# Smoothing factors earlier in SyncE's queue, and five pieces of the last stages moved

## The chip, the cores and the metric

The kernel runs on one core of one Trainium2 chip. The metric is the device time of one execution in microseconds (us). Engines are named as in the profile: PE is the matrix engine (PEld its weight loads), DVE the vector engine, ACT the scalar engine, POOL the GpSimd engine, SP the engine that only issues transfers here (SPq its queue).

## The reference, cut to what matters

Input x is [4, 256, 256] (batch, sequence, feature), and so is the context. Four residual blocks follow one another:

```
x = x + wkv(layernorm(x), context)                 # a scan over the sequence
x = x + quantised_linear(layernorm(x))             # 256 x 256, 8 bit
x = x + L1_xattn(layernorm(x), context)            # below: most of the work
x = x + L1_ffn(layernorm(x))                       # the last layer
```

```
ln_out = ln(h); xq = fp8(clip(ln_out / in_scale))  # one xq for each of q, qx, k, v
q, qx  = ln(xq @ wq), ln(xq @ wqx)                 # 16 heads of 128, 8 groups of 2
k, v   = ln(xq @ wk), xq @ wv                      # 8 groups
kx, vx = ln(context @ w_kv_x[k]), context @ w_kv_x[v]
core   = softmax(q k^T / sqrt(128)) v              # and the same with qx, kx, vx
cat    = fp8(clip(concat(core, xout) / proj_smooth))
x      = x + (cat @ wproj) * scale                 # 4096 features back to 256
```

`L1_ffn` runs along the batch axis of 4: layer norm, a convolution of two steps, SiLU, projections to q, k, v, g, a routed linear attention, a norm by head, a gate, and a projection back.

## The kernel before, in words

**Units.** The attention block is cut into 32 units: unit `u` is batch `u // 8` and group `u % 8` (`b, g = divmod(u, G)`). In each unit two heads of self attention (x = 0) and two of cross attention (x = 1) are computed for two halves (t = 0, 1) of the sequence. Each engine has its own program, a loop over units, and semaphores tie them together. The order of instructions is written by hand.

**PE in iteration u.** `scores(u, 0, 0)` (L625, L626), the second half of the projections of unit u + 1 (`project(u + 1, 1)`, L521 and L529), the other scores, and four times `weigh` (L638: probabilities times values). Between them stand the transposes of unit u + 1 (`turn`, L594), the rough scores from which its row maxima come (`guard`, L611), and the first half of the projections of unit u + 2 (`project(u + 2, 0)`). `turn_outputs(u - 1)` (L652) turns the outputs of the unit before. Once in eight units `project_out` (L662) multiplies the collected outputs with the weights; its second half and the turning of outputs share one PSUM bank, XB, and `residual` on DVE (L1586) reads that bank and frees it.

**DVE in iteration u.** `quantise(u - 1)` (L1577 to L1581), a piece of preparation for the next batch (`early`), `outputs(u, 0, 0)` (L1563 and L1565: divide by the row sum and by the smoothing factors), `normalise(u + 1, 1)` (L1531, L1533), `outputs(u, 0, 1)`, where g is 1 the `residual` of the batch before, another piece of preparation (`middle`), the bf16 copies `halves(u + 1)` (L1542, L1544), `outputs(u, 1, 0)`, the row maxima (`maxima`, L1551), `outputs(u, 1, 1)`, a last piece (`end`), and two more maxima. `weigh` writes all four results of a unit to one bank, OB, so each `weigh` waits until `outputs` has read the one before it (`o_evac`).

**Preparation.** The first two blocks of the next batch run in slices beside the units of the batch before: `ahead(u)` gives batch and step. Step 4 (units 3, 11, 19) adds the first block to x, takes the statistics in `early` and applies them in `middle` (`ln_apply`, L1291). Step 6 (units 5, 13, 21) adds the second block and takes the statistics in `early` (L1349, L1281 to L1286), POOL raises the variance to the power -1/2 (L1121), and `middle` applies it.

**Transfers.** SP issues nearly all of them, in the order of its program, and stands at each wait until it is met. In iteration u it waits for the outputs of unit u - 2, loads the smoothing factors of unit u (`ism`, L366, two buffers), then waits for the projections of unit u and loads the projection weights of unit u + 2 (`WQ`, L341, 1.5 MB, two buffers). The weights come from a DRAM copy, `wq_split`: in the first eight units they are prepared on the side (`weights`, `low_weights`, L492 to L500, L891, L1512) and stored there (L329), and the loads of raw weights (L306, L321) stand in the same queue.

**POOL in iteration u.** `diagonals(u, 0)` (L1175), which `scores(u, 0, 0)` waits for, the powers for the head norms of unit u + 1 (L1161), `diagonals(u, 1)`, the norms of the preparation, and `half(u + 1)` (L1168), which `guard(u + 1, 1)` waits for.

**The end.** The last layer's statistics of three of the four batches (`stats3`, L1635 to L1640, on DVE) stand in iteration 30 behind `outputs(30, 1, 1)`, ahead of the last maxima of unit 31. POOL's `power3` (L1196) stands ahead of `half(31)` in the same iteration. DVE then applies them (`normalise3`, L1646), and PE turns the three results (`turn_inputs3`, L707) between the scores of unit 31, all in bank QB[1], each waiting for ACT's copy (`turned3`, L985) of the one before. `project3` (L724) begins the last layer's projections behind the last `weigh` of unit 31.

Of the kernel before, what the change touches and what calls it, by code (L numbers as in the profile page):

```python
# [7 lines left out]
ALU = mybir.AluOpType  # L8
# [34 lines left out]
def build_program(nc, a, out):  # L43
# [28 lines left out]
    with main:  # L72
# [20 lines left out]
        mhalf = sb("mhalf", [P, 16])  # L93

# [71 lines left out]
        st3 = lb("st3", [P, T8, 6])  # L166
        mv3 = lb("mv3", [P, T8, 2])
        ve3 = lb("ve3", [P, T8])
        pw3 = lb("pw3", [P, T8])
# [74 lines left out]
        T3B, P3A, P3B, OT3B, OUT3B = QB[1], (QB[0], QB[2]), QB[3], (QB[1], SB[1]), (OB, XB)  # L244
# [46 lines left out]
        def _(sp):  # L291
# [39 lines left out]

            def load_weights(u):

                g = u % G
                sp.wait_ge(s["qkv_done"], 4 * (u - 1))
                if u < G:
                    sp.wait_ge(s["wq01_stored"], 32)
                    sp.wait_ge(s["wq_stored"], 16 * (g - 1))
                else:
                    sp.wait_ge(s["wq_stored"], 16 * (G - 2))  # L340
                sp.dma_start(WQ[u % 2][:].bitcast(F32).rearrange("p a k c -> p (a k c)"), wq_dram[g]).then_inc(s[f"wq{u % 2}_loaded"], 16)  # L341
# [13 lines left out]
            sp.wait_ge(s["smooth_stored"], 16)  # L355
            sp.wait_ge(s["xq4_ready"], 4)
# [5 lines left out]
            for u in range(UNITS):  # L362
                g = u % G
                if u >= 2:
                    sp.wait_ge(s["o_evac"], 4 * (u - 1))
                sp.dma_start(ism[:, u % 2], smooth_dram.rearrange("(x f) -> x f", x=2)[:, g * HPG * P:(g + 1) * HPG * P]  # L366
                             .partition_broadcast(P)).then_inc(s[f"ism{u % 2}_loaded"], 16)
                if u + 2 < UNITS:
                    load_weights(u + 2)
                if u == 0:  # L370
                    store_weights(4)
                if u == 1:
                    weights(6)
                if u == 2:
                    store_weights(5)
                    weights(7)
                if u == 3:
                    store_weights(6)
                    load_out_weights(0)
                if u == 4:  # L380
                    store_weights(7)
                if u == 5:
                    load_out_weights(2)
                    load_out_weights(4)
                if u == 6:
                    load_out_weights(6)
                if u and ahead(u) and ahead(u)[1] == 0:
                    b = ahead(u)[0]
                    sp.wait_ge(s["xq4_ready"], 4 * b)
                    sp.dma_start(craw, cv_[b]).then_inc(s["ctx_loaded"], 16)  # L390
# [16 lines left out]
        def _(pe):  # L407
# [293 lines left out]
            def turn_inputs3(l):  # L701

                pe.wait_ge(s["h3_ready"], l + 1)
                pe.wait_ge(*(s["h3T_evac"], l) if l else (s["max_ready"], 4 * UNITS))
                for c in range(KT):
                    for t in range(NT):
                        last = nc.tensor.transpose(T3B[:, (c * NT + t) * P:(c * NT + t + 1) * P],  # L707
                                                   h3[:, l * NT + t, c * P:(c + 1) * P], ident[:])
                last.then_inc(s["h3T_done"], 1)

            def project3(l):

                if l == 0:
                    pe.wait_ge(s["w3_loaded"], 80)
                pe.wait_ge(s["silu_ready"], l + 1)
# [32 lines left out]
            for u in range(UNITS - 1):  # L748
# [39 lines left out]
                for r in round_of(u, 2):  # L788
                    weights(*r)
                guard(u + 1, 1)  # L790
# [5 lines left out]
            turn_inputs3(0)  # L796
            scores(u, 0, 0)
            turn_inputs3(1)
            scores(u, 0, 1)
            turn_inputs3(2)  # L800
# [22 lines left out]
        def _(act):  # L823
# [159 lines left out]
            def turned3(l):  # L983
                act.wait_ge(s["h3T_done"], l + 1)
                A(hT[:, :, l, :], T3B[:].rearrange("p (k t) -> p k t", k=KT), ACT.Copy).then_inc(s["h3T_evac"], 1)  # L985
# [69 lines left out]
            turned3(0)  # L1055
            exps(u, 0, 0)
            turned3(1)
            exps(u, 0, 1)
            turned3(2)
# [36 lines left out]
        def _(pool):  # L1096
# [102 lines left out]
            for u in range(UNITS):  # L1199
# [21 lines left out]
                if u == UNITS - 2:  # L1221
                    power3(0, B - 1, 1)
                if u + 1 < UNITS:
                    half(u + 1)

# [44 lines left out]
        def _(dve):  # L1270
# [32 lines left out]
            def early(b, step):  # L1303
# [43 lines left out]
                if step == 6:  # L1347
                    for t in range(NT):
                        ch.add(v.scalar_tensor_tensor(out=xs[:, b, t, :], in0=hb[:, t, :], scalar=fq[:, 4, t:t + 1],  # L1349
                                                      in1=xs[:, b, t, :], op0=ALU.mult, op1=ALU.add))  # L1350
                    ch.wait()

                    ln_stats(b, 2, 1.0 + EPS, EPS * EPS)
                if step == 7:
                    fp8(b, (0, 1))

# [249 lines left out]
            early(0, 6)  # L1606
# [124 lines left out]
            for u in range(UNITS - 1):  # L1731
# [12 lines left out]
                outputs(u, 0, 1)  # L1744
                if g == 1 and b:
                    residual(b - 1)
                if nb:
                    middle(nb, step)
                for r in round_of(u, 0):
                    low_weights(*r)  # L1750
                halves(u + 1)
                outputs(u, 1, 0)
                maxima(u + 1, 0, 0)
                maxima(u + 1, 0, 1)
                outputs(u, 1, 1)
                for r in round_of(u, 1):
# [3 lines left out]
                if u == UNITS - 2:  # L1760
# [5 lines left out]
                if u == UNITS - 2:  # L1766
                    normalise3(0, B - 1, 1)

# [73 lines left out]
```

## Time and profile before

| | us |
|---|---|
| median of 3 runs | 782.08 |
| lowest and highest | 781.76, 784.39 |
| the profiled execution | 781.98 |
| its span | 780.3 |
| PE busy | 649.8 (83%) |
| DVE busy | 567.3 (73%) |
| ACT busy | 421.1 (54%) |
| POOL busy | 264.5 (34%) |

Span is the time from the first to the last instruction of the core; 1.7 us of the profiled execution lie outside it. Busy shares are means over the whole span. Matmul ends are modelled. A unit takes 16.7 us where no preparation runs beside it, and 17 to 26 us elsewhere.

### The profile page before, as it was taken

Reading aid. Unit: us, or ns where it says so; the run is one execution under the profiler, and the core shown is the slowest. Engines: PE = TensorE matmul, PEld = TensorE weight load, DVE = VectorE, ACT = ScalarE, POOL = GpSimd, SP = SyncE. Lnnn points to the kernel's source line nnn. Section 1 sums busy time; section 2 is a strip of 40 time slices with the busy share of each in tenths; the row PEclk is TensorE's granted clock in tenths of the full one; section 3 lists DMA queues with packets and bytes.
Section 4 is the critical chain, followed back from the end, with each engine's and each line's share of the span. In section 5 each row is a group of like instructions: output and inputs, shape, how many; then the busy total and the mean of one; then the engine's idle time right before and its main releaser. Section 6 shows DMA issues by size and latency. Waiting matters only on the chain.

```text
span 780.3 us, 12837 instructions
## 1 busy us (share of the span) xinstructions
PE 649.8 (83%) x4241; PEld 513.0 (66%) x4279; DVE 567.3 (73%) x1361; ACT 421.1 (54%) x1362; POOL 264.5 (34%) x346
## 2 busy tenths in 40 slices
PE   4258769977889999999899899998998999869444
PEld 2247657755767777877687778776786787646233
DVE  7985558957567757877978588778645666667995
ACT  4156647745657736566665456676645666542221
POOL 3014343323213443434235434343322333224260
PEclk9567999989989999999999999999999999979668
DMA  8157274463456222233232233333421430200001
GB/s 250 54 217 228 96 233 174 179 199 116 164 150 214 96 86 95 98 101 101 100 104 95 83 105 98 95 123 90 152 85 38 148 112 15 81 0 2 0 1 54
DMA packets 33212, 86.47 MB, mean 111 GB/s; under 512 B 2911, under 2 KB 28155, under 8 KB 28283
## 3 DMA queue, kind: packets, MB, share of 16 engines
q1 hardware_dynamic: 32960, 85.63, 33.4%
q8 instruction: 35, 0.57, 0.3%
q14 instruction: 31, 0.25, 0.1%
q10 hardware_dynamic: 186, 0.02, 0.0%
HBM read 71.99 MB, written 13.65 MB: 110 GB/s over the span
## 4 chain that ended last, share of the span: by engine, by line
PE 57%; DVE 24%; DMA 7%; issue 5%; ACT 4%; SPq 1%; POOL 1%; DVEq 0%; POOLq 0%; ACTq 0%
PE bank L638 14%; PE bank L521 12%; PE bank L625 9%; PE bank L529 6%; DMA ism<-smooth_inverse 6%; DVE Cb L1565 4%; PE bank L594 3%; PE bank L662 3%; PE bank L724 2%; PE bank L626 2%; PE bank L611 1%; PE bank L652 1%; DVE ro L1563 1%; DVE stage L1512 1%; DMA wq_split<-stage 1%
## 5 line engine op out<-in xcount | busy, mean ns | idle before, releaser
L638 PEld LDWEIGHTS bank<-V,Pt 128*128 128x128 f32 x1024 | 130.5, 196 | 71.9 <-DVE Cb L1565 60.1
L638 PE MATMUL bank<-V,Pt 128*128 128x129 f32 x1024 | 145.0, 286 | 36.3 <-DVE Cb L1565 34.4
L925 ACT ACTIVATE square<-bank 128x128 bf16<-128x128 f32 x384 | 101.5, 277 | 92.5 <-PE bank L521 54.0
L521 PE MATMUL bank<-WQ,xq 128*128 128x256 f32 (+1 forms) x1024 | 136.7, 286 | 3.9 <-DVE xq L1453 2.7
L521 PEld LDWEIGHTS bank<-WQ,xq 128*128 128x128 f32 x1024 | 127.3, 193 | 17.0 <-DVE nm L1551 9.8
L625 PE MATMUL bank<-QT,KTt 128*128 128x512 f32 x256 | 133.5, 603 | 1.6 <-POOL diag L1175 1.6
L908 ACT ACTIVATE Pt<-bank 128x512 f32<-128x512 f32 x128 | 76.8, 600 | 73.5 <-remote 46.7
L1551 DVE TENSOR_REDUCE nm<-bank 128x2 f32<-128x512 f32 x128 | 82.1, 683 | 45.4 <-PE bank L611 45.3
L1161 POOL TENSOR_TENSOR rs<-ve,mhalf 128x6 f32<-128x6 f32 x64 | 95.0, 1485 | 5.3
L1175 POOL TENSOR_TENSOR diag<-identb,nm 128x512 bf16<-128x512 bf16 x64 | 67.0, 1047 | 71.4 <-DVE nm L1551 71.3
L1563 DVE RECIPROCAL ro<-bank 128x2 f32<-128x2 f32 x128 | 21.7, 169 | 86.3 <-PE bank L638 60.2
L1565 DVE SCALAR_TENSOR_TENSOR Cb<-bank,ro,ism 128x128 bf16<-128x128 f32 x256 | 78.1, 347 | 4.5
L925 ACT ACTIVATION_READ_ACCUMULATOR square<-bank 128x1 f32 x384 | 78.7, 205 | 0.0
L1168 POOL CAST KTh<-KTt 128x256 bf16<-128x256 f32 x32 | 12.7, 396 | 180.4 <-ACT KTt L935 180.4
L529 PE MATMUL bank<-WC,vT 128*128 128x256 f32 x256 | 70.3, 399 | 0.0
L1159 POOL TENSOR_SCALAR ve<-ss 128x6 f32<-128x6 f32 x64 | 18.9, 295 | 126.4 <-ACT square L925 126.4
L935 ACT ACTIVATE QT<-bank,vec 128x512 f32<-128x512 f32 x64 | 50.1, 783 | 16.0 <-PE bank L594 15.9
L1531 DVE TENSOR_TENSOR Qn<-bank,rs 128x512 f32<-128x512 f32 x64 | 43.9, 685 | 19.4 <-POOL rs L1161 19.3
L625 PEld LDWEIGHTS bank<-QT,KTt 128*128 128x128 f32 x256 | 43.1, 192 | 14.7 <-issue 12.4
L594 PE MATMUL bank<-ident,Qn 128*128 128x128 f32 x384 | 52.5, 292 | 0.0
L948 ACT ACTIVATE catT<-bank 128x1024 bf16<-128x1024 bf16 x32 | 32.8, 1025 | 28.4 <-PE bank L652 28.4
L529 PEld LDWEIGHTS bank<-WC,vT 128*128 128x128 f32 x256 | 45.0, 196 | 3.7
(205 smaller groups left out, 1021.7 us busy)
## 6 DMA issues: line engine op xcount, KB each, us to landing
WQ<-wq_split SPq DMA_DIRECT2D x30, 1536.0 KB, 6.8
wq_split<-stage SPq DMA_DIRECT2D x6, 1536.0 KB, 6.4
ism<-smooth_inverse SPq DMA_DIRECT2D x32, 256.0 KB, 4.8
wst<-in_L_xattn_wproj SPq DMA_DIRECT2D x16, 256.0 KB, 3.9
wq_split<-WQ SPq DMA_DIRECT2D x2, 1536.0 KB, 6.1
wst<-in_L_xattn_wq SPq DMA_DIRECT2D x8, 256.0 KB, 4.9
wst<-in_L_xattn_wqx SPq DMA_DIRECT2D x8, 256.0 KB, 5.0
wst<-in_L_xattn_w_kv_x SPq DMA_DIRECT2D x16, 128.0 KB, 4.5
```

The source lines that it names most:

```text
L521: last = nc.tensor.matmul(o[:, o0:o0 + n], xq[b % 2][:, p, k, ts], WQ[u % 2][:, part, k, w0:w0 + n], start=m == 0, stop=m == 2 * KT - 1)
L529: last = nc.tensor.matmul(QB[2 * t + 1][:, 2 * P:4 * P], vT[b % 2][:, k, t * P:(t + 1) * P], WC[:, k, g, :], start=k == 0, stop=k == KT - 1)
L594: last = nc.tensor.transpose(o[:, (j * NT + t) * P:(j * NT + t + 1) * P], Qn[:, t, h, :], ident[:])
L625: nc.tensor.matmul(o[:], KTt[u % 2][:, x, t * P:(t + 1) * P], QT[u % 2][:, x, :], start=True, stop=False)
L638: last = nc.tensor.matmul(OB[:, h * (P + 2):h * (P + 2) + P + 1], Pt[:, x, k, h * S + t * P:h * S + (t + 1) * P], V[u % 2][:, x, k, 0:P + ...
L908: A(Pt[:, x, t], SB[n % 2][:], ACT.Exp, scale=SCALE).then_inc(s["exp_done"], 1)
L925: last = A(square[:, t, h], head(t, h), ACT.Square, accum_out=ss[:, t, h:h + 1])
L935: A(o, i, ACT.Identity, scale=vc(f"L1_xattn_{name}ln_w"), bias=vc(f"L1_xattn_{name}ln_b")).then_inc(s["qt_evac"], 1)
L1161: gp.tensor_tensor(rs[:, t, :], ve[:, t, :], mhalf[:, 0:6], ALU.pow).then_inc(s["rs_ready"], 1)
L1175: gp.tensor_tensor(diag[u % 2][:, x], identb[:].unsqueeze(1).to_broadcast([P, HPG * NT, P]), nm[u % 2][:, x].rearrange("p h t -> p (h t)") ...
L1551: v.tensor_reduce(nm[u % 2][:, x, :, t], GUARD_BANK[t][:].rearrange("p (h t) -> p h t", h=HPG), AX_X, ALU.max, negate=True).then_inc(s["ma ...
L1565: last = v.scalar_tensor_tensor(out=c4[:, t, x, h, :], in0=OB[:, h * (P + 2):h * (P + 2) + P], scalar=ro[:, x, t, h:h + 1], in1=ism[:, u % ...
```

## The change

- **SP.** The load of `ism` becomes a function, `load_smooth`. Units 0 and 1 are loaded right behind the store of the inverse factors, ahead of the stores and loads of weights that stood before them. From then on iteration u loads the factors of unit u + 1 (with the same wait: the outputs of unit u - 1), and the weights of unit u + 2 stand behind that load.
- **DVE, residual.** It moves ahead of `outputs(u, 0, 1)`.
- **DVE, preparation.** At step 6 the addition and the statistics leave `early` and become `add_hidden`, behind `outputs(u, 0, 1)`; at steps 4 and 6 `middle` moves behind `halves(u + 1)`.
- **Last layer.** `stats3` and `power3` of three batches move from iteration 30 to iteration 28, `power3` now behind `half`. `normalise3` moves ahead of the last maxima of unit 31. PE turns the three inputs in iteration 30, ahead of `guard(31, 1)`, the second of them in bank QB[0] and not QB[1]; ACT copies them ahead of the exponentials of unit 31. Four small tiles are allocated for the whole program.

```diff
-            for u in range(UNITS):
-                g = u % G
-                if u >= 2:
-                    sp.wait_ge(s["o_evac"], 4 * (u - 1))
-                sp.dma_start(ism[:, u % 2], smooth_dram...)
+            sp.wait_ge(s["smooth_stored"], 16)
+            load_smooth(0)
+            load_smooth(1)
...
+            for u in range(UNITS):
+                if u and u + 1 < UNITS:
+                    load_smooth(u + 1)
                 if u + 2 < UNITS:
                     load_weights(u + 2)
```

```diff
             def turn_inputs3(l):
                 pe.wait_ge(s["h3_ready"], l + 1)
-                pe.wait_ge(*(s["h3T_evac"], l) if l else (s["max_ready"], 4 * UNITS))
+                if l == 1:
+                    pe.wait_ge(s["qt_evac"], 4 * UNITS)
+                if l >= 2:
+                    pe.wait_ge(s["h3T_evac"], l - 1)
...
+                if u == UNITS - 2:
+                    for l in range(B - 1):
+                        turn_inputs3(l)
                 guard(u + 1, 1)
```

```diff
# POOL
-                if u == UNITS - 2:
-                    power3(0, B - 1, 1)
                 if u + 1 < UNITS:
                     half(u + 1)
+                if u == UNITS - 4:
+                    power3(0, B - 1, 1)
# DVE
                 normalise(u + 1, 1)
-                outputs(u, 0, 1)
                 if g == 1 and b:
                     residual(b - 1)
-                if nb:
+                outputs(u, 0, 1)
+                if nb and step not in (4, 6):
                     middle(nb, step)
+                if nb and step == 6:
+                    add_hidden(nb)
                 for r in round_of(u, 0):
                     low_weights(*r)
                 halves(u + 1)
+                if nb and step in (4, 6):
+                    middle(nb, step)
                 outputs(u, 1, 0)
...
                 outputs(u, 1, 1)
+                if u == UNITS - 2:
+                    normalise3(0, B - 1, 1)
...
-                if u == UNITS - 2:
+                if u == UNITS - 4:
                     stats3(0, B - 1)
                 maxima(u + 1, 1, 0)
```

## Rows read from the trace of the kernel before

**Rows 1.** The page's chain that ended last, shares of the span by line.

```profile
PE bank L638 14%; PE bank L521 12%; PE bank L625 9%; PE bank L529 6%; DMA ism<-smooth_inverse 6%; DVE Cb L1565 4%; PE bank L594 3%; PE bank L662 3%; PE bank L724 2%; PE bank L626 2%; PE bank L611 1%; PE bank L652 1%; DVE ro L1563 1%; DVE stage L1512 1%; DMA wq_split<-stage 1%
```

**Rows 2.** Who waited for whom: us in total, times, longest us.

```profile
DVE ro L1563 <- DMA ism<-smooth_inverse: 24.3, 5, 6.8
...
PE bank L652 <- DVE xs L1586: 5.0, 3, 1.7
```

**Rows 3.** Timeline, DVE, first outputs of units 0, 1, 4, 5, 6: start, us.

```profile
82.56 0.17 DVE L1563 RECIPROCAL ro<-bank 128x2 f32<-128x2 f32 x1 [6.11 <-DMA ism<-smooth_inverse]
...
107.46 0.17 DVE L1563 RECIPROCAL ro<-bank 128x2 f32<-128x2 f32 x1 [4.42 <-DMA ism<-smooth_inverse]
...
168.15 0.17 DVE L1563 RECIPROCAL ro<-bank 128x2 f32<-128x2 f32 x1 [6.80 <-DMA ism<-smooth_inverse]
...
195.71 0.17 DVE L1563 RECIPROCAL ro<-bank 128x2 f32<-128x2 f32 x1 [4.55 <-DMA ism<-smooth_inverse]
...
220.56 0.17 DVE L1563 RECIPROCAL ro<-bank 128x2 f32<-128x2 f32 x1 [2.36 <-DMA ism<-smooth_inverse]
```

**Rows 4.** Timeline, all engines: what came before those outputs in units 0, 4, 6.

```profile
77.08 1.05 PE L638 MATMUL bank<-V,Pt 128*128 128x129 f32 x8
...
162.25 1.05 PE L638 MATMUL bank<-V,Pt 128*128 128x129 f32 x8
...
216.91 1.29 DVE L1453 TENSOR_TENSOR xq<-tmp 128x512 fp32r<-128x512 bf16 x2
```

**Rows 5.** Stretches, PE: length, busy (instructions), granted clock, DMA share, GB/s.

```profile
170.00:176.00 6.00, 4.31 (x23) 0.50 0.02 8
...
218.40:221.40 3.00, 0.06 (x1) 0.88 0.83 323
```

**Rows 6.** Timeline: weight load of unit 7 issued, and its first use.

```profile
191.16 0.32 SPq L341 DMA_DIRECT2D WQ<-wq_split  x1
...
204.07 2.04 PE L521 MATMUL bank<-WQ,xq 128*128 128x256 f32 x16
```

**Rows 7.** DMA issues, weight loads at 191.2 and 97.7: KB, us to landing.

```profile
WQ<-wq_split SPq DMA_DIRECT2D x1, 1536.0 KB, 8.3
...
WQ<-wq_split SPq DMA_DIRECT2D x1, 1536.0 KB, 13.4
```

**Rows 8.** Timeline: projections of unit 30 begin, factors issued (unit 28 ended).

```profile
645.69 2.04 PE L521 MATMUL bank<-WQ,xq 128*128 128x256 f32 x16
...
646.82 0.36 SPq L366 DMA_DIRECT2D ism<-smooth_inverse  x1
```

**Rows 9.** Timeline, unit 9: the residual and PE behind it.

```profile
288.85 0.74 DVE L1586 SCALAR_TENSOR_TENSOR xs<-bank,vec,xs 128x512 f32<-128x512 f32 x1
...
289.74 0.61 PE L652 MATMUL bank<-identb,Cb 128*128 128x128 bf16 x8 [1.66 <-DVE xs L1586]
```

**Rows 10.** Timeline, DVE: norm of step 4 in unit 11, step 6 in 13.

```profile
325.70 0.73 DVE L1291 TENSOR_SCALAR tmp<-xs,lnm,lnr 128x256 f32<-128x256 f32 x2
...
356.33 0.87 DVE L1349 SCALAR_TENSOR_TENSOR xs<-tmp,fq,xs 128x256 f32<-128x256 f32 x2
...
358.31 0.17 DVE L1286 TENSOR_SCALAR lnv<-lnm 128x2 f32<-128x2 f32 x1
...
362.69 0.17 DVE L1563 RECIPROCAL ro<-bank 128x2 f32<-128x2 f32 x1 [0.21 <-PE bank L638]
```

**Rows 11.** Timeline: first scores of unit 29; statistics and power in unit 30.

```profile
648.92 1.02 PE L625 MATMUL bank<-QT,KTt 128*128 128x512 f32 x2
...
680.14 2.05 DVE L1635 BATCH_NORM_STATS2 st<-xs 128x6 f32<-128x256 f32 x6
...
683.02 1.32 POOL L1196 TENSOR_TENSOR pw<-ve,mhalf 128x6 f32<-128x6 f32 x1 [10.36 <-DVE ve L1640]
```

**Rows 12.** Timeline, PE: rough scores of unit 31, first projections of the last layer.

```profile
684.75 1.03 PE L611 MATMUL bank<-KTh,QTh 128*128 128x256 bf16 x4 [5.38 <-POOL KTh L1168]
...
702.16 10.05 PE L724 MATMUL bank<-W,cv 128*128 128x512 f32 x30
```

More of the change, by code:

```diff
@@ L93, in build_program @@
         mhalf = sb("mhalf", [P, 16])
+        st3 = sb("st3", [P, T8, 6])
+        mv3 = sb("mv3", [P, T8, 2])
+        ve3 = sb("ve3", [P, T8])
+        pw3 = sb("pw3", [P, T8])
         rows = [(n, KT) for n in (
@@ L165, in build_program @@
         cs = lb("cs", [P, B, 2, DK3 // 2])
[L166 to L169, printed above, removed]
         h3 = lb("h3", [P, T8, D])
@@ L241, in head @@
             return QB[2 * t][:, h * P:(h + 1) * P] if h < 4 else QB[2 * t + 1][:, (h - 4) * 2 * P:(h - 4) * 2 * P + P]
-        T3B, P3A, P3B, OT3B, OUT3B = QB[1], (QB[0], QB[2]), QB[3], (QB[1], SB[1]), (OB, XB)
+        T3B = (QB[1], QB[0], QB[1], QB[1])
+        P3A, P3B, OT3B, OUT3B = (QB[0], QB[2]), QB[3], (QB[1], SB[1]), (OB, XB)
         def rows3(buffer, l):
@@ L330, in store_weights, with load_smooth @@
                              ).then_inc(s["wq_stored" if g >= 2 else "wq01_stored"], 16)
+            def load_smooth(u):
+                g = u % G
+                if u >= 2:
+                    sp.wait_ge(s["o_evac"], 4 * (u - 1))
+                sp.dma_start(ism[:, u % 2], smooth_dram.rearrange("(x f) -> x f", x=2)[:, g * HPG * P:(g + 1) * HPG * P]
+                             .partition_broadcast(P)).then_inc(s[f"ism{u % 2}_loaded"], 16)
             def load_weights(u):
@@ L362, in _ @@
             for u in range(UNITS):
-                g = u % G
-                if u >= 2:
-                    sp.wait_ge(s["o_evac"], 4 * (u - 1))
-                sp.dma_start(ism[:, u % 2], smooth_dram.rearrange("(x f) -> x f", x=2)[:, g * HPG * P:(g + 1) * HPG * P]
-                             .partition_broadcast(P)).then_inc(s[f"ism{u % 2}_loaded"], 16)
+                if u and u + 1 < UNITS:
+                    load_smooth(u + 1)
                 if u + 2 < UNITS:
@@ L703, in turn_inputs3 @@
                 pe.wait_ge(s["h3_ready"], l + 1)
-                pe.wait_ge(*(s["h3T_evac"], l) if l else (s["max_ready"], 4 * UNITS))
+                if l == 1:
+                    pe.wait_ge(s["qt_evac"], 4 * UNITS)
+                if l >= 2:
+                    pe.wait_ge(s["h3T_evac"], l - 1)
                 for c in range(KT):
                     for t in range(NT):
-                        last = nc.tensor.transpose(T3B[:, (c * NT + t) * P:(c * NT + t + 1) * P],
+                        last = nc.tensor.transpose(T3B[l][:, (c * NT + t) * P:(c * NT + t + 1) * P],
                                                    h3[:, l * NT + t, c * P:(c + 1) * P], ident[:])
@@ L714, in project3 @@
                     pe.wait_ge(s["w3_loaded"], 80)
+                    pe.wait_ge(s["max_ready"], 4 * UNITS)
+                    pe.wait_ge(s["h3T_evac"], 2)
                 pe.wait_ge(s["silu_ready"], l + 1)
@@ L984, in turned3 @@
                 act.wait_ge(s["h3T_done"], l + 1)
-                A(hT[:, :, l, :], T3B[:].rearrange("p (k t) -> p k t", k=KT), ACT.Copy).then_inc(s["h3T_evac"], 1)
+                A(hT[:, :, l, :], T3B[l][:].rearrange("p (k t) -> p k t", k=KT), ACT.Copy).then_inc(s["h3T_evac"], 1)
             def silu3(l):
@@ L1054, in _ @@
             u = UNITS - 1
-            turned3(0)
+            for l in range(B - 1):
+                turned3(l)
             exps(u, 0, 0)
-            turned3(1)
             exps(u, 0, 1)
-            turned3(2)
             exps(u, 1, 0)
@@ L1346, in early, with add_hidden @@
                     ln_stats(b, 1, 1.0, EPS)
[L1347 to L1353, printed above, removed]
                 if step == 7:
                     fp8(b, (0, 1))
+            def add_hidden(b):
+                ch.wait()
+                for t in range(NT):
+                    ch.add(v.scalar_tensor_tensor(out=xs[:, b, t, :], in0=hb[:, t, :], scalar=fq[:, 4, t:t + 1],
+                                                  in1=xs[:, b, t, :], op0=ALU.mult, op1=ALU.add))
+                ch.wait()
+                ln_stats(b, 2, 1.0 + EPS, EPS * EPS)
             def middle(b, step):
@@ L1605, in _ @@
             end(0, 5)
-            early(0, 6)
+            add_hidden(0)
             low_weights(0, 2, HEAD_BANK[0][2])
@@ L1765, in _ @@
                     low_weights(*r)
-                if u == UNITS - 2:
-                    normalise3(0, B - 1, 1)
             u = UNITS - 1
```

3 lines of the change are left out of this document (removed).

## The prediction

> **What bounds the kernel now.** I read the page's chain first. Nearly all of it is PE, but one transfer stands among the PE lines: the load of the smoothing factors, 6% of the span, some 45 us [rows 1]. A 256 KB load has no business on a chain, so the waits come next: DVE waited for it five times, 24.3 us in all, and PE waited three times for the residual [rows 2]. The timeline places the five waits in units 0, 1, 4, 5 and 6 [rows 3], where SP's queue is full of weight stores and raw weights. From unit 7 on no outputs wait for the factors; there PE sets the pace and a plain unit takes 16.7 us. So the first edit is read from the first seven units, the others from the units in which they stand.
>
> **Factors first in the queue.** *What is won.* The wait counts from the moment at which nothing else was missing. In unit 0 the products end at 77.08 + 1.05 = 78.1 and the outputs begin at 82.56: 4.4 us. In unit 4 it is 163.3 and 168.15: 4.8. In unit 6 DVE is through with its own work at 218.2 and goes on at 220.56: 2.4 [rows 3, 4]. In units 1 and 5 DVE came to the wait last, and its whole idle time counts: 4.4 and 4.55 [rows 3]. That is 20.6 bare. With the new order each `ism` has landed a unit earlier (two at about 50 us, the rest at the end of the unit before), so none of it should stay.
>
> *The clock.* After such a wait PE runs at half clock: in 170 to 176 the granted clock was 0.50 (1.2 GHz) with 4.31 us busy, which is 2.2 us of work too much, and a PE idle time of 3.0 us in unit 6 was enough to lower it [rows 5]. ACT and DVE cover part of that, so I take half of the 2.2, 0.9 to 1.1 in units 1, 4 and 6, and 0.2 in unit 0, where ACT's exponentials of the preparation end last anyway.
>
> *What is late next.* The projection weights. Unit 7's were issued at 191.16 [rows 6], landed 8.3 later [rows 7] at 199.5, and are used at 204.07 [rows 6]. The load waits for a store that moves only with the end of unit 4, so unit 5 can win 204.07 - 199.46 = 4.6 us, not more. Unit 3's weights landed 13.4 us after issue, behind a store [rows 7]; by the same count they would be 0.8 late. By unit: 4.6 + (4.4 + 0.9 - 0.8) + (4.8 + 1.1) + 4.6 + (2.4 + 1.1) = 23.1 won. Ends: 17, if the clock gives nothing and the weights take 3 more; 27, if every dip is paid back in full.
>
> *What is queued behind the new wait.* In iteration u the factors of unit u + 1 wait for the end of unit u - 1, and the weight load stands behind them. It used to be issued some 6 us into the iteration before; now it is issued about 0.9 after that unit's end. In the plain stretch unit 28 ended at 646.8 and the projections that need such a load begin 1.1 before a unit's end, that is at 645.69 + 16.7 = 662.4 [rows 8]. That leaves 14.7 us, and the longest of all landings, behind a store, took 13.4 [rows 7]. I cost it at nothing. In the first units the stores and raw weights behind it depend on work later than that wait.
>
> **Residual ahead of the second outputs.** It reads only XB and is ready long before. It ran at 288.85, behind `outputs(u, 0, 1)`, and PE stood 1.66 us until it was done [rows 9]. Now it follows `normalise`, whose last half ends 1.0 us before, while PE is in `weigh`: PE can go on at about 288.7 and not 289.74, 1.1 us each, in units 9, 17 and 25. 3.3 won; ends 0 and 3 x 1.66 = 5.0.
>
> **Preparation norms.** At step 6 the addition and statistics take 358.48 - 356.33 = 2.15 us [rows 10]. They stood before `outputs(u, 0, 0)`, where DVE would have idled for most of it; they cost PE some 0.2. Behind `outputs(u, 0, 1)` DVE is only waiting 0.5 us for ACT's copies, so `halves` comes 1.4 later, then the norm (0.73 [rows 10]) also stands ahead of `outputs(u, 1, 0)`: 2.15 + 0.73 + POOL's power partly hidden. Counted from the end of the second outputs, by the timeline 361.05 and 0.2 earlier than now: statistics to 363.2, copies to 363.95, norm to 364.75, outputs at 364.8 where they were at 362.69 [rows 10]. PE waits for that read, so 2.1 us are lost in each of units 13 and 21; in unit 5 the weights of unit 7 cover it. 4.2 lost; ends 0 (if the slices fall in idle time that I don't see) and 8 (a clock dip in each). At step 4 the norm of 0.73 leaves the idle time in front of the copies and comes to stand before `outputs(u, 1, 0)`: 0.5 in units 3, 11 and 19, 1.5 lost; ends 0 and 2.2.
>
> **Statistics of the last layer in iteration 28.** On DVE they run from 680.14 to 682.94 in iteration 30, power until 684.34 [rows 11]. In iteration 28 they begin when unit 28 ends, 646.8 [rows 8], and are done at 649.6. DVE's last maxima come 0.7 late, which PE hides. But POOL stands in `power3` until 651.0, and behind it in its queue is `diagonals(29, 0)`, for which `scores(29, 0, 0)` waits: it ran at 646.0, now from 651.0 to 652.0. The scores start at 652.1 and not at 648.92 [rows 11]: 3.2 us in which PE has nothing to do, of which some 0.3 come back from waits that it now skips. An idle time of 3.0 us lowered the clock before [rows 5], so I add 1.1 for an even chance of 2.2. 4.0 lost; ends 0.7 and 5.5.
>
> The Trainium skill (TensorE: Matmul & The Clock Gate, Part 1) says that the array falls back to half rate after idling and returns only with sustained work. With the rule taken as certain the term is 5.1 and the sum 1.1 higher; the trace agrees as far as 0.88 in that stretch shows.
>
> **The end.** `guard(31, 1)` stood 5.4 us for POOL's copy, behind `power3`, and ran at 684.75, at half clock [rows 12]. In the new order: `normalise3` on DVE from 680.2 to 682.9 (six instructions, 2.74), PE's three turnings at 681.2, 682.1 and 683.0, `guard` from 683.65, maxima 684.2 to 685.5, `quantise(30)` to 688.3, first outputs of unit 31 at 689.9. Then DVE and PE alternate as before, and `project3` begins at 697.2 and not at 702.16 [rows 12]: 4.9 won with the clock full. PE is nearly idle from 679.4 to 683, so I take off 0.6 for a dip. 4.3 won; ends 2 and 6. All that follows shifts with it. The last layer's weights are loaded long before.
>
> **Sum.** 781.98 (own time; the median, 782.08, is the same within 0.1) - 23.1 - 3.3 + 4.2 + 1.5 + 4.0 - 4.3 = 761.0.
>
> **Rivals.**
> A. *The moved pieces on DVE and POOL cost nothing.* For it: DVE is 73% busy and idles in every unit. Against it: the places in which they now stand have 0.5 us of idle time. Then 9.7 us are not lost: 751.
> B. *The weights take the factors' place.* For it: unit 5's and unit 3's loads are late by my own count, and stores and loads share one queue. If each of the five units keeps half of its wait, 11.5 less is won: 772.
> C. *Clock dips in units 13, 21, 29 and 31.* For it: 3.0 us were enough once. Against it: a wait of 1.66 did not do it [rows 9]. Some 2 us each beyond what is in the sum: 767.
> D. *The weight loads, now behind the wait for the unit's end, are late in every unit.* It decides from 14.7 us of landing on; each of the 22 loads from unit 8 on then costs PE the excess, and from 1.0 us of excess on all 21 us are gone: at 15.9 us, 785. Against it: no landing took more than 13.4, and from unit 8 on nothing else is in the queue.
> E. *The change doesn't do what it says*, the factors still arrive last: then only the rest acts, 784. Against it: the two first loads need only the store of the factors.
>
> **How the numbers follow.** Forecast (756 to 765) 0.56, A 0.12, B 0.15, C 0.12, D 0.03, E 0.02. About 0.3%, 2.3 us, is what a measurement of this kernel can tell from no change. Faster 0.95 (the forecast, A, B, C), same 0.01, slower 0.04 (D and E, nearly). Range 753 to 770: it holds the forecast and C, and half of A and B.
>
> **What would show it.** Right: no idle time of DVE before L1563 put down to `ism`; `wq_split` or L341 as what PE's L521 waits for in units 1 and 5; L652 waiting under 0.7 us in units 9, 17, 25; `outputs(u, 1, 0)` of units 13 and 21 some 2 us later within their unit; a PE idle time of about 3 us ahead of L625 at the start of unit 29; no wait of L611 for POOL. Wrong: the first eight units shorter by under 17 or over 27 us; units 13 and 21 no longer than before; unit 29's scores starting on time; PE waiting for weights in the plain stretch.

## The result, and the profile after

Four runs each, on the same chip: 765.0 us after (762.2 to 765.8), 782.7 before (781.8 to 784.4); ratio 0.977, 95% interval 0.973 to 0.980. The profiled execution took 764.5, its span 762.7, where that of before was 780.3: 17.6 us less, at a granted clock of 0.94. The prediction was 761.0. In the experiments below, three executions that ran far longer than the rest (one of e5, one of e6, one of the kernel before beside them) are left out of the ratios; the medians hold them, which moves none by more than some 0.5 us.

First the page's chain by line (answers to [rows 1]), and then who waited for whom: us in total, times, longest (answers to [rows 2]).

```profile
PE bank L529 13%; PE bank L646 12%; PE bank L633 10%; PE bank L537 6%; DVE Cb L1579 3%; DMA WQ<-wq_split 3%; PE bank L670 3%; PE bank L737 2%; PE bank L602 2%; PE bank L634 2%; DMA wq_split<-stage 2%; PE bank L619 1%; PE bank L660 1%; DVE stage L1526 1%; DVE ro L1577 1%
```

```profile
DVE ro L1577 <- PE bank L646: 64.2, 61, 8.3
...
PE bank L633 <- POOL diag L1187: 4.6, 3, 3.0
...
PE bank L529 <- DMA WQ<-wq_split: 2.8, 2, 1.5
...
PE bank L660 <- DVE xs L1600: 1.6, 3, 0.5
```

The factors' load is gone from both: no DVE idle time is put down to `ism`. The load of the projection weights stands on the chain in their place with 3%, and PE waited for it twice; the list of waits of before has none of it. The residual's wait fell from 5.0 to 1.6 us. PE's 5.4 us for POOL's copy [rows 12] are gone, and there is a new one of 3.0 for POOL's diagonals.

The last reciprocal of a unit (L1563 before, L1577 after) marks the same work in both traces. How much its start moved against the trace of before, less how much the one of the unit ahead moved, is this unit's share (minus is won):

```
unit                        predicted   measured (us, after - before)
0                             -4.6       -4.8
1 to 3                        -4.5+0.5   -3.7  (unit 1 -5.5, unit 2 +1.5, unit 3 +0.3)
4                             -5.9       -6.2
5 and 6                       -8.1       -5.8  (-5.4, -0.4)
7, 8 and all plain units       0          0.0
9, 17, 25 (residual)          -1.1 each  -1.15 each
11, 19 (norm of step 4)       +0.5 each  +0.43 each
13, 21 (step 6)               +2.1 each  +2.05, and +2.99 with +0.45 in unit 22
29 (statistics, power)        +4.0       +6.0
31 (end)                      -4.3       -6.1
behind the last mark            0        +0.2
sum                           -21.0      -17.6
```

Nothing moved outside the units named. The sizes differ in units 2, 6, 21, 29 and 31. Unit 6 comes first: PE's timeline, and its clock (length, busy, granted clock, DMA share, GB/s of each stretch):

```profile
183.05 1.16 PE L646 MATMUL bank<-V,Pt 128*128 128x129 f32 x8 [1.28 <-DVE Cb L1579]
185.71 3.19 PE L529 MATMUL bank<-WQ,xq 128*128 128x256 f32 x16 [1.50 <-DMA WQ<-wq_split]
```

```profile
186.00:188.00 2.00, 2.00 (x13) 2.00 (x13) 0.00 (x0) 0.66 (x5) 0.00 (x0) 0.58 0.48 167
188.00:190.00 2.00, 2.00 (x9) 1.80 (x9) 0.00 (x0) 0.48 (x4) 0.00 (x0) 0.57 0.00 0
```

The five busy times behind the length are PE, PEld, DVE, ACT, POOL. PE waits 1.3 us for DVE's read (step 6's price in unit 5), then 1.5 us for unit 7's weights, and then does sixteen products in 3.19 us that take 2.04 elsewhere, at a granted clock of 0.58 (most of it 1.2 GHz, not 2.4).

The residual in unit 9, ahead of the second outputs (answers to [rows 9]), and step 6 in units 13 and 21 (answers to [rows 10]), timelines:

```profile
267.18 0.74 DVE L1600 SCALAR_TENSOR_TENSOR xs<-bank,vec,xs 128x512 f32<-128x512 f32 x1
267.84 0.16 DVE L1577 RECIPROCAL ro<-bank 128x2 f32<-128x2 f32 x1
268.07 0.61 PE L660 MATMUL bank<-identb,Cb 128*128 128x128 bf16 x8 [0.52 <-DVE xs L1600]
...
339.71 0.87 DVE L1366 SCALAR_TENSOR_TENSOR xs<-tmp,fq,xs 128x256 f32<-128x256 f32 x2
...
342.78 0.79 DVE L1303 TENSOR_SCALAR tmp<-xs,lnm,lnr 128x256 f32<-128x256 f32 x2 [0.39 <-POOL lnr L1133]
343.49 0.16 DVE L1577 RECIPROCAL ro<-bank 128x2 f32<-128x2 f32 x1
344.35 1.16 PE L646 MATMUL bank<-V,Pt 128*128 128x129 f32 x8 [1.28 <-DVE Cb L1579]
...
496.49 0.16 DVE L1577 RECIPROCAL ro<-bank 128x2 f32<-128x2 f32 x1
497.34 1.88 PE L646 MATMUL bank<-V,Pt 128*128 128x129 f32 x7 [1.28 <-DVE Cb L1579]
```

```profile
345.50:348.00 2.50, 2.50 (x21) 2.41 (x20) 0.78 (x3) 1.14 (x8) 1.04 (x1) 1.00 0.09 21
...
497.50:500.00 2.50, 2.50 (x12) 2.50 (x13) 1.48 (x5) 0.00 (x0) 1.04 (x1) 0.50 0.00 0
```

The third outputs of unit 13 start at 343.49, 3.78 after the addition began; the same PE wait of 1.28 us follows in unit 21, 153 us later. In both units a wait of 1.30 us for `halves` (PE L619 <- DVE KTh L1558) stands 1.9 us ahead of it, so the moved pieces make PE wait twice in a row. Behind the one the clock stays at 1.00, behind the other it is 0.50, and seven products take 1.88 us where eight take 1.16. The edit costs 2.06 both times; the clock costs 1.4 more once.

Unit 29, timeline (answers to [rows 11]), and the clock:

```profile
629.08 2.05 DVE L1649 BATCH_NORM_STATS2 st<-xs 128x6 f32<-128x256 f32 x6
...
631.95 1.32 POOL L1208 TENSOR_TENSOR pw<-ve,mhalf 128x6 f32<-128x6 f32 x1 [5.29 <-DVE ve L1654]
633.24 1.04 POOL L1187 TENSOR_TENSOR diag<-identb,nm 128x512 bf16<-128x512 bf16 x1
634.43 2.04 PE L633 MATMUL bank<-QT,KTt 128*128 128x512 f32 x2 [2.97 <-POOL diag L1187]
636.34 3.87 PE L529 MATMUL bank<-WQ,xq 128*128 128x256 f32 x16
```

```profile
634.00:638.00 4.00, 3.57 (x9) 2.29 (x11) 2.05 (x5) 0.60 (x1) 2.78 (x4) 0.50 0.84 354
638.00:642.00 4.00, 4.00 (x18) 3.33 (x18) 1.55 (x3) 1.88 (x13) 0.02 (x1) 0.71 0.03 12
```

The chain is as predicted: statistics, power, diagonals, scores, 2.97 us of PE idle. Behind it PE is busy 3.57 us at 0.50 and 4.00 at 0.71: 3.57 x 0.50 + 4.00 x 0.29 = 2.9 us more than at full clock. Together they are 5.9 of the 6.0.

### The profile page after: what moved, and what is told of

Same layout as the page of the kernel before. It is cut to its first block, busy times and chain, and to the rows that moved or that the text cites. A ratio compares the mean times of both kernels' runs of the same rounds, so it can differ in the third digit from the quotient of the medians.

```text
span 762.7 us, 12837 instructions
## 1 busy us (share of the span) xinstructions
PE 646.1 (85%) x4241; PEld 508.6 (67%) x4279; DVE 568.0 (74%) x1361; ACT 420.1 (55%) x1362; POOL 264.0 (35%) x346
## 4 chain that ended last, share of the span: by engine, by line
PE 56%; DVE 26%; issue 6%; DMA 5%; ACT 5%; POOL 2%; DVEq 0%; SPq 0%; POOLq 0%; ACTq 0%
PE bank L529 13%; PE bank L646 12%; PE bank L633 10%; PE bank L537 6%; DVE Cb L1579 3%; DMA WQ<-wq_split 3%; PE bank L670 3%; PE bank L737 2%; PE bank L602 2%; PE bank L634 2%; DMA wq_split<-stage 2%; PE bank L619 1%; PE bank L660 1%; DVE stage L1526 1%; DVE ro L1577 1%
## 5 line engine op out<-in xcount | busy, mean ns | idle before, releaser
L646 PEld LDWEIGHTS bank<-V,Pt 128*128 128x128 f32 x1024 | 127.5, 193 | 54.9 <-DVE Cb L1579 43.0
L646 PE MATMUL bank<-V,Pt 128*128 128x129 f32 x1024 | 141.2, 281 | 20.7 <-DVE Cb L1579 18.8
L529 PE MATMUL bank<-WQ,xq 128*128 128x256 f32 (+1 forms) x1024 | 140.0, 291 | 6.7 <-DVE xq L1467 2.8
L529 PEld LDWEIGHTS bank<-WQ,xq 128*128 128x128 f32 x1024 | 130.7, 198 | 20.5 <-DVE nm L1565 9.5
L1577 DVE RECIPROCAL ro<-bank 128x2 f32<-128x2 f32 x128 | 21.4, 167 | 66.0 <-PE bank L646 64.2
L602 PE MATMUL bank<-ident,Qn 128*128 128x128 f32 x384 | 48.5, 278 | 0.0
L619 PE MATMUL bank<-KTh,QTh 128*128 128x256 bf16 x256 | 39.8, 279 | 9.3 <-DVE KTh L1558 9.3
```

The source lines that it names most:

```text
L529: last = nc.tensor.matmul(o[:, o0:o0 + n], xq[b % 2][:, p, k, ts], WQ[u % 2][:, part, k, w0:w0 + n], start=m == 0, stop=m == 2 * KT - 1)
L602: last = nc.tensor.transpose(o[:, (j * NT + t) * P:(j * NT + t + 1) * P], Qn[:, t, h, :], ident[:])
L646: last = nc.tensor.matmul(OB[:, h * (P + 2):h * (P + 2) + P + 1], Pt[:, x, k, h * S + t * P:h * S + (t + 1) * P], V[u % 2][:, x, k, 0:P + ...
```

## The experiments

Each group of runs has runs of the kernel before beside it on the same chip; their medians are 784.05, 783.43 and 783.65 (e1 to e4, e5 to e8, e9 and e10). "By units" is the comparison of the table above, with the same trace of before. A trace is one execution, and need not be the one at the median.

**e1, the factors' loads alone.** The kernel before, and in SyncE's program:

```diff
+            load_smooth(0)
+            load_smooth(1)
...
-                if u >= 2:
-                    sp.wait_ge(s["o_evac"], 4 * (u - 1))
-                sp.dma_start(ism[:, u % 2], smooth_dram...)
+                if u and u + 1 < UNITS:
+                    load_smooth(u + 1)
```

> The kernel before with one edit: the smoothing factors' loads issued a unit earlier, the two first ones right behind the store of the factors. Theory (the head's gain is this edit's alone): the units 0 to 6 come out 20.5 us shorter, as in the changed kernel, nothing changes behind them: 782.1 - 20.5 = 761.6, no wait of DVE for the factors. Rival (the moved norms of units 3 and 5 took part in it, hidden behind the late weights of unit 7): 23 us shorter here, 759. Rival (weight loads, now behind the wait for the unit's end, cost something in the plain units): over 764, with PE waiting for weights after unit 7.

759.4 us, ratio 0.969 (0.967 to 0.970): 24.6 less. By units -24.9 in units 0 to 6 and 0.0 in each from 7 to 30 (and +1.15 in unit 31, where the stretch at half clock lies 2.3 us later in the work than before). That is 4.4 more than in the changed kernel. Units 3 and 5 account for 1.4 of it (-0.3 and -6.3 without the moved norms, +0.3 and -5.4 with them), unit 2 for 0.5, and unit 6 for 2.4: there PE waited only 0.7 us for unit 7's weights and the clock stayed full:

```profile
182.91 2.06 PE L528 MATMUL bank<-WQ,xq 128*128 128x256 f32 x16 [0.68 <-DMA WQ<-wq_split]
```

The time is the 759 of the first rival, but the moved norms are only 1.4 of the difference; the rest is late weights and clock. So the edit's gain is its own, and the weight loads, now behind a wait, cost nothing in the plain units.

**e2, everything but the factors.** The changed kernel with that edit taken back.

> The changed kernel with the factors' loads put back where they were, all other edits kept. Theory: the 24 us of waits for the factors are back, and the other edits together cost what the comparison by units gave, -3.4 (residual) + 0.9 (step 4) + 5.5 (step 6) + 6.0 (unit 29) - 6.1 (end) = +2.9 against the kernel before: 785, of which the head gives none. Rival (the norms of units 3 and 5 are hidden behind the factors' waits, and the clock's losses in units 21 and 29 come only with the shifted times of the changed kernel): 779 to 781.

785.3 us, ratio 1.002 (1.000 to 1.004). DVE waits for the factors again:

```profile
DVE ro L1574 <- DMA ism<-smooth_inverse: 27.8, 5, 7.3
```

By units the other edits give -1.14 (three times), +0.44 (twice), +2.06 in unit 21 but +2.98 in unit 13 with +0.45 in unit 14, +4.7 in unit 29, -5.3 at the end: +2.3 together. This execution (788.0) also lost 2.6 in the head against the one of before, with 27.8 us of waits for the factors where that had 24.3. By the ratio the other edits were worth nothing, or cost up to 3 us: what two of them won, the others gave back. The half clock behind step 6 has changed places with the unit that was spared in the changed kernel. The rival, that these losses need the shifted times, falls.

**e3, the preparation norms back.** The changed kernel, with `add_hidden` behind `early` and `middle` ahead of `halves`:

```diff
                 if nb:
                     early(nb, step)
+                if nb and step == 6:
+                    add_hidden(nb)
...
-                if nb and step not in (4, 6):
+                if nb:
                     middle(nb, step)
-                if nb and step == 6:
-                    add_hidden(nb)
...
-                if nb and step in (4, 6):
-                    middle(nb, step)
```

> The changed kernel with step 6's addition and statistics and the norms of steps 4 and 6 back in their old places on DVE (step 6's before the first outputs, the norms before the halves). Theory (they cost 5.5 us in units 13 and 21 and 0.9 in 11 and 19, and nothing in unit 5, where the weights of unit 7 come last): 6.4 us less than the changed kernel, 758.5, unit 21 without a stretch at half clock. Rival A (unit 21's half clock has another cause than the 2.1 us of waiting): 4.9 less, 760. Rival B (unit 5 pays 2.1 too, because the store of unit 7's weights moves with it): 8.5 less, 756.5.

756.1 us, ratio 0.964 (0.963 to 0.966). By units 13, 21, 22, 11 and 19 are 0.0 against before: the cost was this move's, all of it. The spans differ by 6.6 us (762.7 and 756.1), as the theory has it; the two ratios, 0.977 and 0.964, by 9.5, with 2.5 and 1.4 of uncertainty. By the time alone rival B (756.5) is nearer. Of its 2.1 in unit 5 the trace has 0.9 (-6.3, not -5.4), and unit 6 gave it up again (+0.4, not -0.4), at half clock behind 2.3 us of waiting for the weights.

**e4, POOL's power one iteration later.** In POOL's loop of the changed kernel:

```diff
-                if u == UNITS - 4:
+                if u == UNITS - 3:
                     power3(0, B - 1, 1)
```

> The changed kernel with POOL's power of the last layer's variances one iteration later (29, behind its last copy), the statistics on DVE left in iteration 28. Theory (the 6.0 us lost in unit 29 are POOL's diagonals standing behind the power, and the half clock which that idle time brought): PE waits under 0.3 us for the diagonals in unit 29, no half clock there, 5.3 to 6.0 less than the changed kernel, 759. Rival A (the half clock has another cause): 3.0 less, 762. Rival B (it is DVE's 2.85 us of statistics in front of the last maxima that PE waits for): under 1.5 less, 763.5.

756.5 us, ratio 0.966 (0.964 to 0.968), 2.5 less than expected. Unit 29, timeline:

```profile
623.90 1.04 POOL L1187 TENSOR_TENSOR diag<-identb,nm 128x512 bf16<-128x512 bf16 x1 [1.71 <-DVE nm L1565]
624.60 2.05 DVE L1649 BATCH_NORM_STATS2 st<-xs 128x6 f32<-128x256 f32 x6
...
626.82 1.02 PE L633 MATMUL bank<-QT,KTt 128*128 128x512 f32 x2
...
628.05 2.06 PE L529 MATMUL bank<-WQ,xq 128*128 128x256 f32 x16
```

The diagonals no longer stand behind the power, PE waits for nothing and stays at full clock; unit 29 is +0.25, the whole price of the statistics on DVE. 5.7 us were the place of one POOL instruction. Until unit 28 this program is the changed kernel itself, so its trace is a second look at the same code: unit 6 is -3.3 here and not -0.4, units 21 and 22 together +2.07 and not +3.44. Here the weights of unit 7 came 0.2 us late:

```profile
184.13 2.07 PE L529 MATMUL bank<-WQ,xq 128*128 128x256 f32 x16 [0.20 <-DMA WQ<-wq_split]
```

**e5 and e10, both repairs.** e3's and e4's edits together, twice.

> The changed kernel with both repairs: POOL's power in iteration 29, the preparation norms in their old places. Theory (the terms add up, each in its own units): head -24.9 (with the weights of unit 7 landing in 8 us), residual -3.45, unit 29 +0.3, end -6.1 against the kernel before: 782.1 - 34.2 = 748. Rival A (unit 6's 2.9 us at half clock come back because those weights land in over 9 us): 751. Rival B (the repairs share their gain): 753, no better than the better of the two alone.

> The kernel with both repairs once more, for a profile in which the chip isn't throttled throughout. Theory (terms add up): against the kernel before, the span is 25 us shorter behind unit 8 where no stretch at half clock falls behind a late weight load, up to 4.4 less where one does; -3.4, +0.3 and -6.0 to -6.6 behind that; 748 to 753. Rival (the repairs share something): units 9 to 31 differ from those of the runs with only one more edit.

753.7 us, ratio 0.962 (0.960 to 0.965), and 752.7, 0.960 (0.957 to 0.963). Only e10's profile is read, with a span of 751.0. By units: head -21.7, residual -1.15 three times, unit 29 +0.26, end -5.2; the sum is -30.1. That is 4.1 short of e5's theory, 0.9 of it at the end (half clock, see below) and 3.2 in the head: in unit 6 the weights came 1.8 us late and the products ran at half clock:

```profile
184.51 3.29 PE L529 MATMUL bank<-WQ,xq 128*128 128x256 f32 x16 [1.77 <-DMA WQ<-wq_split]
```

The two times lie nearer to rival B's 753 than to rival A's 751, so the units have to decide, and they do: 7 to 28 are e3's and 29 is e4's, within 0.02. That is rival A: the terms add up, and the late weights and the clock decide on the rest.

**e6, the last layer's edits alone,** on the kernel before, with the power in iteration 29.

> The kernel before with the last layer's edits alone: statistics in iteration 28, POOL's power in 29, normalisation and turns in iteration 30. Theory (the end's gain is taken from PE's wait for POOL's copy behind the power, whatever the head does): +0.3 in unit 29, -6.1 at the end, nothing elsewhere: 776.3. Rival (part of the end's gain in the changed kernel is the clock, which stood low from unit 29 on in none of these): -4.9 at the end, 777.5.

777.9 us, ratio 0.993 (0.991 to 0.996), 5.5 less. By units +0.27 in unit 29, -6.6 at the end, 0.0 in units 7 to 28, so the rival's -4.9 falls. But +2.4 in the head, where nothing was edited: DVE's waits for the factors are the same (24.2 us in five), and the clock stayed low longer behind them. The stretch 111 to 114, before and in e6:

```profile
111.00:114.00 3.00, 3.00 (x30) 2.98 (x28) 1.08 (x5) 2.34 (x5) 0.10 (x1) 0.93 0.37 94
```

```profile
111.00:114.00 3.00, 3.00 (x16) 3.00 (x16) 0.78 (x3) 1.38 (x3) 0.00 (x0) 0.50 0.20 55
```

In 176 to 179 and 200 to 203 it is the same: 0.95 and 0.97 before, 0.50 in e6.

**e7, unit 3's weights first.** Both repairs, and:

```diff
                 if u == 0:
+                    load_weights(3)
                     store_weights(4)
```

(and no longer in iteration 1; the same in e9).

> The kernel with both repairs, and the load of unit 3's weights issued ahead of the fifth store and of the factors of unit 2, behind which it landed 13.9 us after issue. Theory (that load is what PE waits for in unit 1): it lands within 10 us, PE's wait of 1.3 goes, 1.0 to 1.7 us less than the kernel with both repairs, 746.7. Rival (store and load share the 16 DMA engines whichever is issued first): no difference, still over 12 us to landing. Rival (the fifth store, now later, makes unit 4's weights late): 1 us or more slower, PE waiting in unit 2 or 3.

749.2 us, ratio 0.957 (0.955 to 0.958). The load was issued at 75.69, not 92.9: it had only stood behind waits that were not its own. It took 11.1 us and not 10, but landed 18 us before it was wanted; unit 2 is 0.0 and not the +1.4 of e10, with no PE wait:

```profile
105.19 2.04 PE L530 MATMUL bank<-WQ,xq 128*128 128x256 f32 x16
```

Unit 6 was late again (2.2 us of waiting, clock 0.50 in 186 to 188, -0.1). The edit explains these 1.4 us; the median is 4.5 below e5's and 3.6 below e10's, and what the other 2 to 3 are is open.

**e8, the raw output weights held back.** Both repairs, and ahead of `load_out_weights(2)`:

```diff
+                    sp.wait_ge(s["wq1_loaded"], 48)
```

> The kernel with both repairs, and SyncE waits for the landing of unit 7's weights before it issues the raw output weights of iteration 5, so that this load has the DMA engines to itself. Theory A (the raw weights in the queue make it late, 7.5 to 9.2 us to landing, and so decide on the half clock of unit 6): it lands in under 7.3 us, PE's wait before unit 7's projections is gone, no half clock there, 0.3 to 3 us less than the kernel with both repairs (in which that stretch fell either way). Theory B (the landing doesn't depend on them; the plain units' load took 9.6 with nothing but the factors beside it): 7.5 to 9.2 as before and no difference, or, if the raw weights are now late for their rounds, 1 to 3 us slower.

749.5 us, ratio 0.957 (0.955 to 0.959). Unit 7's load (KB, us to landing) without the raw weights, and in the changed kernel with them issued 2 us behind it:

```profile
WQ<-wq_split SPq DMA_DIRECT2D x1, 1536.0 KB, 8.3
```

```profile
WQ<-wq_split SPq DMA_DIRECT2D x1, 1536.0 KB, 9.2
```

In e1 and e4 it took 7.5 and 8.0 with the raw weights in flight, so 8.3 without them is no gain. Contention with them is not what makes it late: theory B. It was not alone, though: the factors' load of unit 6, issued 5.2 us ahead of it, was in flight until 182.9, and no run takes that away. That such company counts is seen in the plain units. The page's line for this load, kernel before (the factors some 10 us ahead) and changed kernel (0.5 us ahead):

```profile
WQ<-wq_split SPq DMA_DIRECT2D x30, 1536.0 KB, 6.8
```

```profile
WQ<-wq_split SPq DMA_DIRECT2D x30, 1536.0 KB, 9.6
```

In e6, with the old order, it is 6.7. So the first edit made most weight loads 3 us slower to land, where nothing waits for them. PE waited 1.4 us, at full clock behind it. The time is lower than e5's and e10's all the same; I can't say why, since the trace shows unit 2 at +4.3 (that load took 15.1 us) and a sum of -30.6, hardly better than e10's.

**e9, unit 7's weights without the trip through DRAM.** e7, and in iteration 4 (iteration 5 then loads neither unit 6's factors nor unit 7's weights):

```diff
+                    sp.wait_ge(s["w_evac"], 8 * 8)
+                    sp.wait_ge(s["wl_ready"], 3 * 8)
+                    sp.wait_ge(s["qkv_done"], 4 * 6)
+                    sp.dma_start(WQ[1]..., stage...).then_inc(s["wq1_loaded"], 16)
+                    load_smooth(6)
                     store_weights(7)
```

> The kernel with both repairs and the early load of unit 3's weights, and unit 7's weights copied from the staging buffer straight into their place once unit 5's projections are done (about 170), instead of through the store (168.7, landed 174.3) and the load behind it (landed 183.4); the store, for the later batches, goes behind. Theory (the trip through DRAM is what PE waits for before unit 7's first projections, and that wait brings the half clock of unit 6): the copy lands by 180, PE goes on at 181.2 and not at 183.4, no half clock in 183 to 189, 2.2 to 5 us less than the version before it: 745. Rival A (the copy inside SBUF is slower, 13 us or more): no gain. Rival B (PE then waits for something else in units 5 and 6, ACT's or DVE's copies of raw weights): under 1 us.

746.5 us, ratio 0.953 (0.951 to 0.954), the fastest of all. The copy's issue, first use and landing, and the clock in the stretch that was at half:

```profile
168.83 0.53 SPq L393 DMA_DIRECT2D WQ<-stage  x1
...
181.13 2.04 PE L536 MATMUL bank<-WQ,xq 128*128 128x256 f32 x16
```

```profile
WQ<-stage SPq DMA_DIRECT2D x1, 1536.0 KB, 7.0
```

```profile
182.00:184.00 2.00, 2.00 (x16) 1.85 (x15) 0.23 (x1) 1.14 (x8) 0.48 (x1) 1.00 0.53 180
```

The copy landed at 175.8. PE waits for nothing and goes on at 181.13 where 181.2 was expected; unit 6 is -3.8. The late weights and their half clock are one cause, the store and the load in sequence, and with it removed all of the head's gain is there: -26.7, and -36.5 up to the last outputs of unit 31.

## Why the prediction was right, and where its terms were off

- *Factors.* Right, place by place: units 0, 1, 4 within 0.3 us of their own terms with the weights set apart. That the weights are late next was right too, and for the named reason: unit 7's load waits for a store that moves only with unit 4 (170.81 to 176.42). The term gave 23.1; seven traces give 20.5 (changed kernel) to 24.9 (e1), and e9, without the late weights, 26.7. What was missing is that this new wait can lower the clock as the old ones did: unit 5 was held to 4.6 because of the wait, but for unit 6, where its half clock falls, the full 3.5 stood in the sum, and 0.4 was measured. "0.8 late" for unit 3's weights was 1.0 to 1.7, and 4.3 in e8.
- *Residual.* 1.1 predicted, 1.14 to 1.16 in eight traces.
- *Preparation norms.* 2.1 predicted for step 6, 2.06 in each case without a fall of the clock; 0.5 for step 4, 0.43 in units 11 and 19. That unit 5 hides them behind the weights was right only roughly: e1's units 5 and 6 are together -9.1, e4's -8.7, 0.4 less. Rival A (they cost nothing) is refuted by e3, and its argument, DVE's 27% of idle time, with it.
- *Statistics in iteration 28.* The mechanism was right, the size was not, and with unit 6's this is the step that failed: "I add 1.1 for an even chance of 2.2". The wait was 2.97 (predicted 2.9); the clock cost 2.9, not 1.1. In e3 it was the same (+6.1), in e2 the unit lost 4.7: all three traces lost at least 1.7 beyond the wait. Over all traces, of nine PE waits of 2.6 to 3.6 us from unit 4 to 29, eight had a stretch at half clock that began within 2 us of them. The ninth, in unit 6 of e2, is the longest but one:

```profile
225.39 1.16 PE L643 MATMUL bank<-V,Pt 128*128 128x129 f32 x8 [3.45 <-DVE Cb L1576]
```

```profile
225.40:229.00 3.60, 3.60 (x36) 3.59 (x37) 1.65 (x5) 1.97 (x4) 0.00 (x0) 1.00 0.18 74
```

  So a fall was likelier than even here, and not certain. The Trainium skill (TensorE: Matmul & The Clock Gate, Part 1), that the array falls back to half rate after idling and needs sustained work to return, would have made the term 5.1; the trace of unit 29 agrees with its direction and puts the size at 6.0, and e2's unit 6 shows a wait without a fall.
- *The end.* 4.3 predicted, 6.1 measured; 5.2 to 6.6 in the others. PE idled 1.6 us there (669.35, below), and the last turns and first scores ran at half clock. The clock in 671 to 674, and in e9 at the same work (653 to 656):

```profile
671.00:674.00 3.00, 3.00 (x10) 1.53 (x9) 1.84 (x4) 0.88 (x2) 0.50 (x1) 0.50 0.00 0
```

```profile
653.00:656.00 3.00, 2.78 (x12) 1.19 (x10) 2.52 (x4) 1.44 (x4) 1.19 (x5) 1.00 0.00 0
```

```profile
669.35 2.32 PE L718 MATMUL bank<-ident,h 128*128 128x128 f32 x12 [1.62 <-DVE h L1660]
671.46 1.06 PE L619 MATMUL bank<-KTh,QTh 128*128 128x256 bf16 x4
...
684.38 6.18 PE L737 MATMUL bank<-W,cv 128*128 128x512 f32 x18
```

  The same wait of 1.6 us stands there in nine traces. In three of them (e6, e8, e9) the clock stayed full, and all three have -6.6; in the six with a fall it is -5.2 to -6.2. So the fall cost 0.5 here, and the 0.6 taken off for it was owed. What was mis-sized is the rest: shifted by unit 30's 11.65, the first outputs start at 689.6 even with the fall (predicted 689.9 without one), and the alternation of DVE and PE behind them took 0.9 less than it was given, so L737 starts at 696.0 and not at 697.9.
- *Rivals.* C (more falls of the clock, 767) is nearest to what this profile shows: unit 21 had one (1.4), unit 29's and the end's cost 2.9 and 0.5, unit 13 had none, and unit 6, which C does not name, had one. B (weights in the factors' place) holds for two units, at 1.3 and 1.5 us, not for five. D did not come: on plain units the loads land 9.4 to 9.9 us after issue, and PE never waited. Its argument that nothing else is in the queue there was wrong (the factors are, see e8), only the margin was large. E is refuted by e1.
- *The sum* was 3.4 too low: +2.1 (head, with unit 3's norm), -0.15 (residual), -0.15 (step 4 in units 11 and 19), +1.3 (step 6), +2.0 (unit 29), -1.8 (end), +0.2 behind the last mark, up to rounding. The three large ones on the slow side are the clock's, with the late weights; in e4's trace the same code's units 6, 21 and 22 are 4.3 us shorter.

## What to carry to other kernels

A load that stands on the chain can be late only because of what is ahead of it in its queue: look at what its own waits would allow (e7: 17 us earlier) and at who else's waits it inherits. Before an instruction that waits is put into an engine's queue, name the next instruction behind it and who needs that: one 1.3 us POOL operation, moved by an iteration, was worth 5.7 us. And on this kernel a PE wait can have two prices, its length and up to as much again at half clock: in some executions for waits of 1.3 to 2.4 us, in eight of nine cases around 3. Pieces moved "to fill idle time" need a gap as long as they are.

## What the hardware showed that was not expected

- The same work loses or keeps the clock at short waits, and no trace shows what decides. Behind the two waits of step 6 (1.30 and 1.28 us): half clock in 2 of 6 cases (units 13 and 21 of three traces). Behind the 1.6 us at the end: in 6 of 9. Behind unit 7's late weights: full clock after waits of 0.2, 0.7 and 1.4 us, half clock after 1.5, 1.8, 2.2 and 2.3; behind unit 3's, full after 0.8 to 1.4 and half after 2.4. But behind the residual's 1.66 us (kernel before, e1, e6) it stayed full in 9 of 9, so the length of one wait does not decide alone. Units 6, 21 and 22 of the changed kernel and of e4, the same code up to there, differ by 4.3 us through late weights and clock, more than some of the edits are worth; comparing unit by unit takes it out.
- A copy of 1.5 MB inside SBUF took 7.0 us to land (e9), a load of the same size from DRAM 7.5 to 15.2 in the head. In plain units it took 9.6 with the factors' load issued 0.5 us before it, and 6.6 with that load some 10 us before (medians, changed kernel and before), so the copy is not faster by itself. With a store issued 0.9 us before it took 13.9.
- One of DVE's 16-bit operations takes 0.43 us in 28 units of the changed kernel and 1.14 in four, and in each of these four POOL's diagonals began 0.3 us before it. The quantisation of units 29, 22 and 30:

```profile
657.50 0.43 DVE L1592 TENSOR_SCALAR Ce<-Cb 128x1024 uint16<-128x1024 uint16 x1
```

```profile
523.88 1.15 POOL L1187 TENSOR_TENSOR diag<-identb,nm 128x512 bf16<-128x512 bf16 x1 [4.54 <-DVE nm L1565]
524.17 1.15 DVE L1592 TENSOR_SCALAR Ce<-Cb 128x1024 uint16<-128x1024 uint16 x1
...
673.50 1.15 POOL L1187 TENSOR_TENSOR diag<-identb,nm 128x512 bf16<-128x512 bf16 x1 [4.67 <-DVE nm L1565]
673.78 1.14 DVE L1592 TENSOR_SCALAR Ce<-Cb 128x1024 uint16<-128x1024 uint16 x1
```

  DVE's operation ends some 0.3 us behind POOL's each time. The next one, L1593, took 1.08 once, beside POOL's writing of its table of cosines, and 0.43 everywhere else. That POOL is the cause was not tested by a run of its own. The Trainium skill (GPSIMD Engine Reference, 1. Specifications) says that GpSimd shares its SBUF interfaces with VectorE and that instructions in VectorE's two-port mode or with two SBUF inputs collide with it; these rows agree that the two collide, and do not show VectorE's mode.
